# A decoder layer on one core: the last batch's projection, norms, gate and experts tile by tile, in a part of their own behind the slots

## The chip, the core and the metric

The kernel runs on one core of a Trainium2 chip. The core has five engines that run their own instruction streams and meet only through semaphores: PE (TensorE, matrix multiplies into the eight banks of PSUM), DVE (VectorE), ACT (ScalarE), POOL (GpSimd) and SP (SyncE, which here only issues DMAs). The metric is the device time of one execution in microseconds; lower is better.

## The reference

The layer computes, on `x` and `ctx` of 8 batches x 512 tokens x 512 features, a two-part self attention, a cross attention over `ctx`, and a gated pair of experts, each followed by a residual sum and a norm:

```
x = layernorm(x + self_attention(x))
x = layernorm(x + cross_attention(ctx, ctx, x))       # ... @ Wo.T + bo at its end
x = layernorm(x + ffn(x))

def ffn(x):
    weights = softmax(x @ gate_w)                      # 8 experts
    fw, fidx = top_k(weights, 2)
    e0, e1 = silu(x @ w0.T + b0), silu(x @ w1.T + b1)
    return e0 * fw[:, 0:1] * (fidx[:, 0:1] == 0) + e1 * fw[:, 1:2] * (fidx[:, 1:2] == 1)
```

For the change only the last lines of the second step and the third step matter: the output projection of cross attention, the second norm ("ln2"), the gate (8 logits a token, a softmax, and whether expert 0 came first and expert 1 second), the two experts, the third norm ("ln3") and the store.

## The kernel before, in words

The kernel has three phases: self attention, a memory phase, and the cross phase. A batch is four tiles of 128 tokens; attention goes through 32 groups (8 batches x 4 groups of 4 heads), each 16 **slots** long. A slot is one 128x512 block of scores: PE makes it (L1350), ACT takes its exponential (L1569), POOL adds four of them up (L1792), PE weighs the values (L1382); 22 slots ahead PE makes the scores again for the row maxima (L1322), which DVE takes (L1332). All engines' code is written slot by slot by a loop over `CROSS_SLOTS`, and the order on each engine is that of the slots: there is no scheduler.

Everything behind attention is put into the slots of the following batch. `behind(n)` says for slot n which batch has which of its own later steps there: projection from slot 12 of its 64, ln2 applied at 31, transposes at 35, gate at 39, logits at 44, experts from 48 (8 **units**, one for each tile and expert, 3 slots each), ln3's statistics from 62, its factors at 81, applied at 83, stored at 87. These steps share banks 6 and 7; the attention steps use the other six.

The last batch (batch 7) has no attention after it to lie beside. Its steps come in `CROSS_SLOTS` past the 512th slot, where only they and the last steps of batch 6 are left, still in the same slot order and still in banks 6 and 7:

- projection, one tile after another, on PE: a bias matmul (L1429), then four chunks of `cy` by `wo` (L1449, fp32, two instructions a chunk). The last chunk's `cy` is the output of the last group's division on DVE (L1640, L1647). PE waits for it before the first tile
- DVE adds each tile to `cx` (L1667) and takes its statistics (L138, L140). ln2's factors are made by POOL once for all four tiles (L146 to L152), behind the fourth tile's statistics; then ACT applies them to the four tiles (L157)
- transposes on PE (L1461) by feature chunk, each of which needs all four tiles; ACT rounds each to its high part (L1584), DVE takes the low part (L1674)
- gate: the 8 gate columns are the stationary operand, the transposed tokens move (`triple`, L163 to L165, 12 matmuls of 8x512); ACT copies the logits (L1589), PE turns them (L1474), DVE makes masks and weights in 15 small instructions for all four tiles (L1699 to L1735), with an exponential on ACT between them (L1592)
- experts: a unit is a bias matmul and 12 matmuls of 128x512 (L1500). ACT takes tanh (L1598), DVE makes the silu product and with it frees the bank (L1684), ACT weighs it by the gate (L1603), POOL adds it to the tokens (L1772)
- ln3: statistics by tile on DVE, factors for all four tiles on POOL, four applies on ACT (L157), one store of the whole batch, 1024 KB (L1845), and SP's wait for it (L1892).

## Time and profile before

| | us |
|---|---|
| median of three runs | 1899.1 |
| lowest and highest of them | 1894.32, 1899.45 |
| profiled execution, its own time | 1899.85 |
| its span, first to last instruction | 1898.0 |
| PE busy in the span | 1752.7 (92%) |
| DVE, ACT, POOL busy | 1268.1, 973.5, 1084.8 |
| granted clock of PE, mean | 0.966 |

The profile is of one execution. A busy share is an average over the whole span; the digits of the page's 40 slices (47 us each) say that PE is at 9 tenths and more nearly throughout and falls to 6 in the last slice, and the chain that ended last goes through PE for 72% of the span. A row of the timeline gives a start, a duration, the engine, the line and, in brackets, how long the engine stood idle before it and what ended that. The duration of a row with a count is from the first start to the last end. A matmul's duration holds the time that it takes to run through the array, so two that start 0.23 us apart have rows of 0.4 us: the pace is read from starts.

### The profile page before, as it was taken

To read this page: it belongs to the slowest core of one execution; us is meant where nothing else is said; L and a number is where in the kernel's file an instruction comes from. 1 tells how busy PE (TensorE), PEld (TensorE's weight loads), DVE (VectorE), ACT (ScalarE), POOL (GpSimd) and SP (SyncE) were. 2 spreads that over 40 slices of the span, in tenths; PEclk is the share of its full clock that TensorE was granted. 3 is DMA by queue.
4 is the path that set the end of the run, shared out by engine and by line. 5 is a ranking of instruction groups with operands and counts; after the bars stand their busy time and mean duration, and the time that the engine had idled before them with its cause. 6 is when DMAs were issued, how large, how long until landed. Compare 5 with 4: busy or idle time off the path is not lost.

```text
span 1898.0 us, 29834 instructions
## 1 busy us (share of the span) xinstructions
PE 1752.7 (92%) x10442; PEld 1092.6 (58%) x10442; DVE 1268.1 (67%) x2747; ACT 973.5 (51%) x1893; POOL 1084.8 (57%) x741
## 2 busy tenths in 40 slices
PE   5999999999999889999988899999999999999986
PEld 4666666666666467777743355464554546455444
DVE  4677676766767567666867666766677676676632
ACT  3555555555555433333355365655556565555543
POOL 2556455565554645554567567666756756766552
PEclk9999999999999879999989899999999999999998
DMA  6455554554645444566436333444344244343100
GB/s 190 134 156 151 140 157 134 155 153 131 165 124 142 143 159 159 185 191 196 133 119 157 94 95 90 112 117 110 92 117 101 79 117 117 89 102 99 48 23 22
DMA packets 166496, 237.21 MB, mean 125 GB/s; under 512 B 21318, under 2 KB 72518, under 8 KB 166348
## 3 DMA queue, kind: packets, MB, share of 16 engines
q1 hardware_dynamic: 166348, 235.31, 44.7%
q8 instruction: 84, 1.38, 0.3%
q14 instruction: 64, 0.52, 0.1%
HBM read 91.57 MB, written 41.94 MB: 70 GB/s over the span
## 4 chain that ended last, share of the span: by engine, by line
PE 72%; DVE 9%; ACT 5%; DMA 5%; POOL 4%; issue 3%; SPq 2%; POOLq 0%; ACTq 0%; DVEq 0%
PE bank L1500 9%; PE bank L163 7%; PE bank L164 6%; PE bank L165 6%; PE bank L1449 5%; PE bank L1382 5%; PE bank L258 5%; PE bank L1350 5%; PE bank L1322 4%; PE bank L313 4%; PE bank L300 4%; POOL cross_added L1792 3%; DVE bank L1640 2%; PE bank L278 2%; DVE bank L497 2%
## 5 line engine op out<-in xcount | busy, mean ns | idle before, releaser
L1332 DVE TENSOR_REDUCE cross_negmax<-bank 128x1 f32<-128x512 f32 x512 | 342.4, 679 | 213.1 <-PE bank L1322 209.1
L1569 ACT ACTIVATE cpt<-bank 128x512 f32<-128x512 f32 x512 | 299.9, 595 | 214.7 <-PE bank L1350 211.5
L484 DVE CUSTOM_DVE_ANT_0 bank<-bank,future 128x128 f32<-128x128 f32 (+3 forms) x512 | 247.0, 489 | 190.5 <-PE bank L300 189.7
L372 ACT ACTIVATE pt<-bank 128x256 f32<-128x256 f32 (+3 forms) x512 | 219.7, 438 | 269.9 <-PE bank L258 264.7
L1792 POOL TENSOR_TENSOR cross_added<-cross_added,cpt 128x2048 f32<-128x2048 f32 x64 | 292.1, 4565 | 56.4 <-ACT cpt L1569 56.2
L1322 PE MATMUL bank<-cqk 96*128 96x512 f32 x512 | 262.6, 517 | 24.2 <-DMA cqk<-cstage 12.1
L1792 POOL TENSOR_TENSOR cross_added<-cpt,cpt 128x2048 f32<-128x2048 f32 x32 | 146.5, 4578 | 185.9 <-ACT cpt L1569 185.9
L1350 PE MATMUL bank<-cqk 98*128 98x512 f32 x512 | 229.1, 448 | 25.5 <-ACT cpt L1569 18.1
L548 POOL TENSOR_SCALAR_AFFINE_SELECT pt<-pt 128x512 f32<-128x512 f32 x128 | 81.4, 636 | 272.8 <-ACT pt L372 272.7
L258 PE MATMUL bank<-qk 98*128 98x256 f32 (+2 forms) x512 | 182.8, 360 | 20.3 <-ACT pt L372 18.4
L163 PE MATMUL bank<-xt_hi,w_hi 128*128 128x512 f32 x384 | 169.4, 441 | 18.4 <-DVE w_lo L442 15.6
L1350 PEld LDWEIGHTS bank<-cqk 98*128 98x128 f32 x512 | 98.6, 193 | 147.1 <-ACT cpt L1569 68.4
L300 PE MATMUL bank<-qk 96*128 96x256 f32 (+2 forms) x512 | 165.4, 327 | 5.0 <-DMA qk<-stage 4.9
L258 PEld LDWEIGHTS bank<-qk 98*128 98x128 f32 x512 | 97.8, 193 | 99.8 <-ACT pt L372 74.0
L164 PE MATMUL bank<-xt_hi,w_lo 128*128 128x512 f32 x384 | 153.6, 400 | 0.0
L165 PE MATMUL bank<-xt_lo,w_hi 128*128 128x512 f32 x384 | 152.6, 397 | 0.0
L1640 DVE RECIPROCAL bank<-bank 128x128 f32<-128x128 f32 x128 | 121.9, 955 | 41.9 <-PE bank L1415 41.9
L1322 PEld LDWEIGHTS bank<-cqk 96*128 96x128 f32 x512 | 99.3, 196 | 80.6 <-DVE cross_negmax L1332 33.9
L1382 PE MATMUL bank<-cpt,cv 128*32 128x512 f32 x1024 | 140.7, 623 | 0.0
L1449 PE MATMUL bank<-wo,cy 128*128 128x512 f32 x256 | 134.7, 616 | 0.0
L1772 POOL TENSOR_TENSOR x<-x,tanh 128x512 f32<-128x512 f32 x64 | 82.4, 1287 | 85.4 <-ACT tanh L1603 84.3
L497 DVE RECIPROCAL bank<-bank 128x128 f32<-128x128 f32 x128 | 122.1, 958 | 8.8 <-PE bank L278 8.8
(172 smaller groups left out, 3463.8 us busy)
## 6 DMA issues: line engine op xcount, KB each, us to landing
qk<-stage SPq DMA_DIRECT2D x384, 128.0 KB, 2.3
cqk<-cstage SPq DMA_DIRECT2D x384, 128.0 KB, 2.3
scratch_memory<-memory SPq DMA_DIRECT2D x32, 512.0 KB, 3.8
ma<-scratch_memory SPq DMA_DIRECT2D x32, 512.0 KB, 3.9
raw<-in_x_t SPq DMA_DIRECT2D x32, 256.0 KB, 2.7
v<-in_x SPq DMA_DIRECT2D x32, 256.0 KB, 3.3
scratch_y_ar<-y_ar SPq DMA_DIRECT2D x32, 256.0 KB, 2.2
my_ar<-scratch_y_ar SPq DMA_DIRECT2D x32, 256.0 KB, 4.6
```

The costliest lines, as they stand in the source:

```text
L163: pe.matmul(out, a[0], b[0], start=first, stop=False)
L164: pe.matmul(out, a[1], b[0], start=False, stop=False)
L165: return pe.matmul(out, a[0], b[1], start=False, stop=last)
L258: pe.matmul(bank[:, 0:SEQ - q0], kq[0:98, 1, j, first:first + P], kq[0:98, 0, j, q0:SEQ], start=True, stop=True).then_inc(s.pe_st, 1)
L300: pe.matmul(bank[:, 0:max(keys, 256)], kq[0:96, 0, j, tile_of(qt)], kq[0:96, 1, j, 0:max(keys, 256)], start=True, stop=True).then_inc(s.pe ...
L484: dve.tensor_tensor_reduce(out=scores, in0=scores, in1=sh.future[:, SEQ - P * (qt + 1):SEQ], scale=-1.0, scalar=-NEG, op0=ALU.add, op1=ALU ...
L1322: pe.matmul(max_bank(sh, m)[:, :], kq[0:96, 0, jm, tile_of(qt)], kq[0:96, 1, jm, :], start=True, stop=True).then_inc(s.pe_mx, 1)
L1332: dve.reduce_max(s.negmax[gm % 2][:, col:col + 1], max_bank(sh, m)[:, :], AX, negate=True).then_inc(s.dve_max, 1)
L1350: pe.matmul(sh.bank[2 + n % 2][:, :], kq[0:98, 1, j, tile_of(kt)], kq[0:98, 0, j, :], start=True, stop=True).then_inc(s.pe_st, 1)
L1382: done = pe.matmul(sh.bank[4][rows_of(j), :], s.v[g % 2][:, kt, rows_of(j)], s.pt[step % 3][:, j, :], start=(kt == 0), stop=(kt == TILES - ...
L1569: act.activation(s.pt[step % 3][:, j, :], sh.bank[2 + n % 2][:, :], ACT.Exp, scale=SCALE_CROSS).then_inc(s.act_exp, 1)
L1792: pool.tensor_tensor(s.added[:, :, :], old[:, :, :], s.pt[step % 3][:, :, :], ALU.add).then_inc(s.pool_add, 1)
```

## The change

Batch 7 no longer has steps in the slots: `behind` leaves it out, and `CROSS_SLOTS` ends where batch 6 is through (its store). Behind the loop each engine gets a piece of its own for batch 7 (`tail_tensor`, `tail_scalar`, `tail_vector`, `tail_gpsimd`, and the stores in `cross_sync`):

- the projection's four tiles go to banks 0 to 3, and the first two do their first three chunks before their fourth
- adding, statistics, factors (`factors_of_tile`), apply and transposes are per tile; the normed tiles go to a buffer of their own, `x3`, in the place of a key and query stack that is free by then; the transposes use banks 4 and 5, the units banks 6 and 7
- the gate has its operands turned round: the transposed tokens are the stationary operand and the 8 gate columns move, so the logits come out with tokens on partitions, in the bank of that tile's projection. The copy of the logits and their transposes go. There are 12 such matmuls a tile, 48 in all
- the 15 gate instructions on DVE and the exponential on ACT are done for each tile, on a quarter of the columns
- ln3 is per tile, and each tile is stored by itself (256 KB, four stores).

The gate's helpers take a bank, a first tile and a number of tiles now; for the other batches they do what they did. The load of `cx` stands in the same slot as before.

```diff
+    def factors_of_tile(self, pool, b, k):
+        n, ks = 4 * (b + k) + 1, slice(k, k + 1)
+        pool.wait_ge(self.vec, 8 * b + 2 * k + 2)
+        if k == 0:
+            pool.wait_ge(self.applied, TILES * b)
+        pool.tensor_scalar(self.rstd[:, ks], self.mv[:, ks, 1], EPS, None, ALU.add).then_inc(self.root, 1)
+        pool.wait_ge(self.root, n + 1)
+        pool.tensor_tensor(self.rstd[:, ks], self.rstd[:, ks], self.power[:, ks], ALU.pow).then_inc(self.root, 1)
+        pool.wait_ge(self.root, n + 2)
+        pool.tensor_tensor(self.shift[:, ks], self.mv[:, ks, 0], self.rstd[:, ks], ALU.mult).then_inc(self.root, 1)
+        pool.wait_ge(self.root, n + 3)
+        pool.tensor_scalar(self.shift[:, ks], self.shift[:, ks], -1.0, None, ALU.mult).then_inc(self.root, 1)
+    def apply_tile(self, act, b, k, out, r):
+        act.wait_ge(self.root, 4 * (b + k) + 5)
+        act.activation(out, r, ACT.Identity, bias=self.shift[:, k:k + 1],
+                       scale=self.rstd[:, k:k + 1]).then_inc(self.applied, 1)
...
-CROSS_SLOTS = range(SLOTS_BEHIND[LAST + 7][1], NS + 2 * BATCH_SLOTS)
+CROSS_SLOTS = range(SLOTS_BEHIND[LAST + 7][1], NS + 25)
...
+LAST_FREE = (NG - 3) % 3
+        self.x3 = Place(nc, ATTENTION + LAST_FREE * STACK_BYTES, TOP)("x3", [P, TILES, DIM])
...
+LAST_BATCH = BATCH - 1
-    return [(bb, r + more) for bb, more in ((b - 1, 0), (b - 2, BATCH_SLOTS)) if 0 <= bb < BATCH]
+    return [(bb, r + more) for bb, more in ((b - 1, 0), (b - 2, BATCH_SLOTS)) if 0 <= bb < LAST_BATCH]
...
-def cross_gate_first(dve, s, sh, b):
+def cross_gate_first(dve, s, bank, at, k0=0, tiles=TILES):
+    n, ks = GATE_OPS * at, slice(k0, k0 + tiles)
+    logits, beats = gate_scratch(bank, 0, tiles), gate_column(bank, 0, tiles)
...
-    sp.wait_ge(s.out_stored, 16 * BATCH)
+    for k in range(TILES):
+        sp.wait_ge(s.ln3.applied, TILES * LAST_BATCH + k + 1)
+        sp.dma_start(s.t["out"][LAST_BATCH, tile_of(k), :], s.x3[:, k, :]).then_inc(s.out_stored, 16)
+    sp.wait_ge(s.out_stored, 16 * (LAST_BATCH + TILES))
...
+    b = n // BATCH_SLOTS - 1
+    if n % BATCH_SLOTS == 1 and b >= 0:
+        if b >= 1:
+            sp.wait_ge(s.ln2.applied, TILES * b)
+        else:
+            sp.wait_ge(sh.memory_done, 4)
+        sp.wait_ge(second.x1_stored[b % 3], 16 * (b // 3 + 1))
+        sp.dma_start(s.x1[:, :, :], t["x1"][b].rearrange("(k p) d -> p k d", p=P)).then_inc(s.x1_landed, 16)
     for b, slot in behind(n):
-        if slot == 1:
-            if b >= 1:
-                sp.wait_ge(s.ln2.applied, TILES * b)
-            else:
-                sp.wait_ge(sh.memory_done, 4)
-            sp.wait_ge(second.x1_stored[b % 3], 16 * (b // 3 + 1))
-            sp.dma_start(s.x1[:, :, :], t["x1"][b].rearrange("(k p) d -> p k d", p=P)).then_inc(s.x1_landed, 16)
...
+def tail_tensor(pe, s, cw, sh):
+    pe.wait_ge(s.act_exp, NS)
+    pe.wait_ge(s.dve_max, NS)
+    for k in (0, 1):
+        tail_project(pe, s, cw, sh, k, range(GROUPS - 1))
+    for k in (0, 1):
+        tail_project(pe, s, cw, sh, k, (GROUPS - 1,))
+    tail_project(pe, s, cw, sh, 2, range(GROUPS))
+    tail_transposed(pe, s, sh, 0)
+    tail_project(pe, s, cw, sh, 3, range(GROUPS))
+    tail_transposed(pe, s, sh, 1)
+    for k in range(TILES):
+        tail_gate(pe, s, cw, sh, k)
+        for i in range(2):
+            tail_expert(pe, s, cw, sh, 2 * k + i)
+        if k + 2 < TILES:
+            tail_transposed(pe, s, sh, k + 2)
+def tail_project(pe, s, cw, sh, k, chunks):
+    b = LAST_BATCH
+    for c in chunks:
+        if c == 0:
+            cross_bias(pe, cw, sh.bank[k], 0)
+        pe.wait_ge(s.dve_norm, (TILES + 1) * (GROUPS * b + c + 1))
+        done = pe.matmul(sh.bank[k][:, :], s.y[:, (GROUPS * b + c) % (GROUPS + 1), tile_of(k)], cw.wo[:, c, :],
+                         start=False, stop=(c == GROUPS - 1))
+        if c == GROUPS - 1:
+            done.then_inc(s.pe_po, 1)
+def tail_transposed(pe, s, sh, k):
+    pe.wait_ge(s.ln2.applied, TILES * LAST_BATCH + k + 1)
+    if k == 0:
+        pe.wait_ge(s.act_raw, NG)
+    elif k == 1:
+        pe.wait_ge(s.dve_norm, (TILES + 1) * NG)
+    else:
+        pe.wait_ge(s.dve_x2t, GROUPS * LAST_BATCH + k - 1)
+    for c in range(GROUPS):
+        done = pe.transpose(sh.bank[4 + k % 2][:, tile_of(c)], s.x3[:, k, tile_of(c)], sh.ident[:, :])
+    done.then_inc(s.pe_x2t, 1)
+def tail_gate(pe, s, cw, sh, k):
+    pe.wait_ge(s.dve_x2t, GROUPS * LAST_BATCH + k + 1)
+    pe.wait_ge(s.dve_po, TILES * LAST_BATCH + k + 1)
+    for c in range(GROUPS):
+        done = triple(pe, sh.bank[k][:, 0:EXPERTS], (s.x2t_hi[:, c, tile_of(k)], s.x2t_lo[:, c, tile_of(k)]),
+                      (cw.gate_hi[:, c, :], cw.gate_lo[:, c, :]), c == 0, c == GROUPS - 1)
+    done.then_inc(s.pe_gate, 1)
+def tail_expert(pe, s, cw, sh, u):
+    k, i = divmod(u, 2)
+    bank = sh.bank[6 + u % 2]
+    pe.wait_ge(s.dve_u, UNITS * LAST_BATCH + u - 1)
+    cross_bias(pe, cw, bank, 1 + i)
+    for c in range(GROUPS):
+        done = None
+        for x, w in ((s.x2t_hi, s.e_hi), (s.x2t_lo, s.e_hi), (s.x2t_hi, s.e_lo)):
+            done = pe.matmul(bank[:, :], x[:, c, tile_of(k)], w[:, i, c, :], start=False,
+                             stop=(c == GROUPS - 1 and w is s.e_lo))
+    done.then_inc(s.pe_ex, 1)
+def tail_scalar(act, s, sh):
+    b = LAST_BATCH
+    act.wait_ge(s.pe_st, NS)
+    act.wait_ge(s.pe_mx, NS)
+    for k in range(TILES):
+        s.ln2.apply_tile(act, b, k, s.x3[:, k, :], s.x1[:, k, :])
+        if k in (1, 2):
+            tail_high(act, s, sh, k - 1)
+    for k in range(TILES):
+        act.wait_ge(s.dve_gate, GATE_OPS * (b + k) + GATE_FIRST)
+        act.activation(gate_scratch(sh.bank[k], 1, 1), s.ge[:, k:k + 1, :], ACT.Exp).then_inc(s.act_gate, 1)
+        tail_tanh(act, s, sh, 2 * k)
+        tail_weigh(act, s, 2 * k)
+        tail_tanh(act, s, sh, 2 * k + 1)
+        if k + 2 < TILES:
+            tail_high(act, s, sh, k + 2)
+        if k >= 1:
+            s.ln3.apply_tile(act, b, k - 1, s.x3[:, k - 1, :], s.x3[:, k - 1, :])
+        tail_weigh(act, s, 2 * k + 1)
+    s.ln3.apply_tile(act, b, TILES - 1, s.x3[:, TILES - 1, :], s.x3[:, TILES - 1, :])
+def tail_high(act, s, sh, k):
+    act.wait_ge(s.pe_x2t, GROUPS * LAST_BATCH + k + 1)
+    if k == 0:
+        act.wait_ge(s.pe_ex, UNITS * LAST_BATCH)
+    act.activation(s.x2t_hi[:, :, tile_of(k)], sh.bank[4 + k % 2][:, :].rearrange("p (c q) -> p c q", q=P),
+                   ACT.Copy).then_inc(s.act_x2t, 1)
+def tail_tanh(act, s, sh, u):
+    n = UNITS * LAST_BATCH + u
+    act.wait_ge(s.pe_ex, n + 1)
+    act.wait_ge(s.pool_x2, n - 1)
+    act.activation(s.tanh[u % 2][:, :], sh.bank[6 + u % 2][:, :], ACT.Tanh, scale=0.5).then_inc(s.act_tanh, 1)
+def tail_weigh(act, s, u):
+    k, i = divmod(u, 2)
+    act.wait_ge(s.dve_u, UNITS * LAST_BATCH + u + 1)
+    act.wait_ge(s.dve_gate, GATE_OPS * (LAST_BATCH + k + 1))
+    act.activation(s.tanh[i][:, :], s.tanh[i][:, :], ACT.Copy, scale=s.w[i][:, k:k + 1]).then_inc(s.act_w, 1)
+def tail_vector(dve, s, sh):
+    b = LAST_BATCH
+    dve.wait_ge(s.x1_landed, 16 * (b + 1))
+    for k in range(TILES):
+        dve.wait_ge(s.pe_po, TILES * b + k + 1)
+        dve.tensor_tensor(s.x1[:, k, :], sh.bank[k][:, :], s.x1[:, k, :], ALU.add).then_inc(s.dve_po, 1)
+        dve.wait_ge(s.dve_po, TILES * b + k + 1)
+        s.ln2.statistics(dve, b, k, s.x1[:, k, :])
+        if k >= 2:
+            tail_low(dve, s, sh, k - 2)
+    for k in range(TILES):
+        dve.wait_ge(s.pe_gate, b + k + 1)
+        cross_gate_first(dve, s, sh.bank[k], b + k, k, 1)
+        cross_gate_weights(dve, s, sh.bank[k], b + k, UNITS * b, k, 1)
+        tail_silu(dve, s, sh, 2 * k)
+        if k >= 1:
+            tail_statistics(dve, s, k - 1)
+        tail_silu(dve, s, sh, 2 * k + 1)
+        if k + 2 < TILES:
+            tail_low(dve, s, sh, k + 2)
+    tail_statistics(dve, s, TILES - 1)
+def tail_low(dve, s, sh, k):
+    dve.wait_ge(s.act_x2t, GROUPS * LAST_BATCH + k + 1)
+    dve.tensor_tensor(s.x2t_lo[:, :, tile_of(k)], sh.bank[4 + k % 2][:, :].rearrange("p (c q) -> p c q", q=P),
+                      s.x2t_hi[:, :, tile_of(k)].bitcast(F32), ALU.subtract).then_inc(s.dve_x2t, 1)
+def tail_silu(dve, s, sh, u):
+    tanh = s.tanh[u % 2]
+    dve.wait_ge(s.act_tanh, UNITS * LAST_BATCH + u + 1)
+    dve.scalar_tensor_tensor(out=tanh[:, :], in0=tanh[:, :], scalar=1.0, in1=sh.bank[6 + u % 2][:, :],
+                             op0=ALU.add, op1=ALU.mult).then_inc(s.dve_u, 1)
+def tail_statistics(dve, s, k):
+    dve.wait_ge(s.pool_x2, UNITS * LAST_BATCH + 2 * k + 2)
+    s.ln3.statistics(dve, LAST_BATCH, k, s.x3[:, k, :])
+def tail_gpsimd(pool, s):
+    b = LAST_BATCH
+    for k in range(TILES):
+        s.ln2.factors_of_tile(pool, b, k)
+    for u in range(UNITS):
+        x = s.x3[:, u // 2, :]
+        pool.wait_ge(s.act_w, UNITS * b + u + 1)
+        pool.wait_ge(s.pe_x2t, GROUPS * b + u // 2 + 1)
+        if u % 2 == 1:
+            pool.wait_ge(s.pool_x2, UNITS * b + u)
+        pool.tensor_tensor(x, x, s.tanh[u % 2][:, :], ALU.add).then_inc(s.pool_x2, 1)
+        if u >= 2 and u % 2 == 0:
+            s.ln3.factors_of_tile(pool, b, u // 2 - 1)
+    s.ln3.factors_of_tile(pool, b, TILES - 1)
```

PE, from the projection of batch 7 to its first expert. Before (`cy` attention output by chunk, `x_176` the normed tokens, `exp_hi` and `x2t_hi` weights and transposed tokens):

```order
L1429 MATMUL bank<-bias_rows,bias_ones 128x512 [waits dve_cross_norm,dve_u]
L1449 MATMUL bank<-wo,cy 128x512 x4
...
L1429 MATMUL bank<-bias_rows,bias_ones 128x512 [waits dve_cross_norm,dve_po]
L1449 MATMUL bank<-wo,cy 128x512 x4
L1461 MATMUL bank<-ident,x_176 128x128 [waits dve_po,ln2_applied]
L1461 MATMUL bank<-ident,x_176 128x128 x3
...
L163 MATMUL bank<-x2t_hi,gate_hi 8x512 [waits dve_x2t]
...
L1474 MATMUL bank<-ident,logits_t 128x8 [waits dve_x2t,act_lt]
L1474 MATMUL bank<-ident,logits_t 128x8 x3
L1429 MATMUL bank<-bias_rows,bias_ones 128x512 [waits act_lt]
```

The same place in the changed kernel (`x_177` is `x3`):

```order
L1459 MATMUL bank<-bias_rows,bias_ones 128x512 [waits dve_cross_max,act_cross_exp]
L1951 MATMUL bank<-wo,cy 128x512 [waits dve_cross_norm] x3
L1459 MATMUL bank<-bias_rows,bias_ones 128x512
L1951 MATMUL bank<-wo,cy 128x512 [waits dve_cross_norm] x5
L1459 MATMUL bank<-bias_rows,bias_ones 128x512
L1951 MATMUL bank<-wo,cy 128x512 [waits dve_cross_norm] x4
L1966 MATMUL bank<-ident,x_177 128x128 [waits act_cross_raw,ln2_applied]
L1966 MATMUL bank<-ident,x_177 128x128 x3
...
L1966 MATMUL bank<-ident,x_177 128x128 [waits dve_cross_norm,ln2_applied]
...
L182 MATMUL bank<-gate_hi,x2t_hi 128x8 [waits dve_po,dve_x2t]
```

The first tile's transposes stand between the third and the fourth tile's projection, and the gate and two units of a tile follow before the next-but-one tile is transposed.

ACT, from the last tile's exponential on. Before:

```order
L1598 ACTIVATE tanh_161<-bank 128x512 [waits pool_x2,pe_ex]
L1603 ACTIVATE tanh_161<-tanh_161,gate_w_172 128x512 [waits dve_gate,dve_u]
L1598 ACTIVATE tanh_162<-bank 128x512 [waits pool_x2,pe_ex]
L1603 ACTIVATE tanh_162<-tanh_162,gate_w_173 128x512 [waits dve_gate,dve_u]
L157 ACTIVATE x_176<-x_176,ln_shift,ln_rstd 128x512 [waits ln3_root]
L157 ACTIVATE x_176<-x_176,ln_shift,ln_rstd 128x512 x3
```

The changed kernel:

```order
L2004 ACTIVATE bank<-gate_exp 128x8 [waits dve_gate]
L2028 ACTIVATE tanh_161<-bank 128x512 [waits pool_x2,pe_ex]
L2035 ACTIVATE tanh_161<-tanh_161,gate_w_172 128x512 [waits dve_gate,dve_u]
L2028 ACTIVATE tanh_162<-bank 128x512 [waits pool_x2,pe_ex]
L170 ACTIVATE x_177<-x_177,ln_shift,ln_rstd 128x512 [waits ln3_root]
L2035 ACTIVATE tanh_162<-tanh_162,gate_w_173 128x512 [waits dve_gate,dve_u]
L170 ACTIVATE x_177<-x_177,ln_shift,ln_rstd 128x512 [waits ln3_root]
```

The apply of the tile before, with its wait for POOL's factors, now stands between the last unit's tanh and its weighing.

## Rows read from the trace of the kernel before

**Rows 1.** Stages of the end: length, busy us (instructions) by engine, clock, DMA share

```profile
1828.00:1843.00 15.00, 14.89 (x36) 6.75 (x36) 6.71 (x14) 3.65 (x5) 2.96 (x5) 1.00 0.18 70
1843.00:1849.70 6.70, 0.00 (x0) 0.00 (x0) 1.57 (x3) 2.92 (x4) 1.70 (x4) 0.74 0.00 0
1849.70:1852.00 2.30, 1.97 (x8) 1.57 (x8) 0.40 (x1) 0.84 (x3) 0.00 (x0) 0.50 0.00 0
...
1884.00:1898.00 14.00, 0.00 (x0) 0.00 (x0) 2.35 (x5) 4.24 (x6) 3.38 (x6) 0.61 0.19 75
```

**Rows 2.** Timeline of PE, from the last unit of batch 6 to the last matmul

```profile
1826.40 0.40 PE L1500 MATMUL bank<-exp_lo,x2t_hi 128*128 128x512 f32 x1
1828.09 0.47 PE L1429 MATMUL bank<-bias_rows,bias_ones 128*128 128x512 f32 x1 [1.30 <-DVE cy L1647]
1831.43 0.79 PE L1429 MATMUL bank<-bias_rows,bias_ones 128*128 128x512 f32 x1
...
1835.09 0.79 PE L1429 MATMUL bank<-bias_rows,bias_ones 128*128 128x512 f32 x1
...
1862.67 0.39 PE L1429 MATMUL bank<-bias_rows,bias_ones 128*128 128x512 f32 x1
...
1883.58 0.40 PE L1500 MATMUL bank<-exp_lo,x2t_hi 128*128 128x512 f32 x1
```

**Rows 3.** Timeline of PE, short matmuls at full clock, in earlier stages

```profile
703.80 0.60 PE L869 MATMUL bank<-ident,my_ar 128*128 128x128 f32 x4
...
707.70 0.83 PE L836 MATMUL bank<-e,ka_t 128*128 128x128 f32 x6
...
1111.10 0.41 PE L1474 MATMUL bank<-ident,logits_t 8*128 8x8 f32 x4
```

**Rows 4.** Timeline of DVE: fourth add, first and last gate instruction, last statistics

```profile
1843.02 0.69 DVE L1667 TENSOR_TENSOR cx<-bank,cx 128x512 f32<-128x512 f32 x1 [2.02 <-PE bank L1449]
...
1859.65 0.19 DVE L1699 TENSOR_REDUCE gate_max<-bank 128x4 f32<-128x32 f32 x1 [3.98 <-PE bank L1474]
...
1861.83 0.23 DVE L1735 TENSOR_TENSOR gate_w<-bank,gate_keep 128x4 f32<-128x4 f32 x2
...
1887.46 0.69 DVE L138 BATCH_NORM_STATS2 ln_stats<-x 128x6 f32<-128x512 f32 x1 [1.31 <-POOL x L1772]
```

**Rows 5.** Timeline of ACT: ln2, gate, last unit, ln3

```profile
1846.78 2.93 ACT L157 ACTIVATE x<-cx,ln_shift,ln_rstd 128x512 f32<-128x512 f32 x4 [8.17 <-POOL ln_shift L152]
...
1860.89 0.20 ACT L1592 ACTIVATE bank<-gate_exp 128x32 f32<-128x32 f32 x1 [1.74 <-DVE gate_keep L1716]
...
1884.01 0.60 ACT L1598 ACTIVATE tanh<-bank 128x512 f32<-128x512 f32 x1 [0.94 <-PE bank L1500]
1885.36 0.72 ACT L1603 ACTIVATE tanh<-tanh,gate_w 128x512 f32<-128x512 f32 x1 [0.76 <-DVE tanh L1684]
1890.44 2.92 ACT L157 ACTIVATE x<-x,ln_shift,ln_rstd 128x512 f32<-128x512 f32 x4 [4.36 <-POOL ln_shift L152]
```

**Rows 6.** Timeline of POOL: last adds of batch 6 and 7, ln3's factors

```profile
1829.38 1.26 POOL L1772 TENSOR_TENSOR x<-x,tanh 128x512 f32<-128x512 f32 x1 [1.73 <-ACT tanh L1603]
...
1883.14 1.28 POOL L1772 TENSOR_TENSOR x<-x,tanh 128x512 f32<-128x512 f32 x1 [1.73 <-ACT tanh L1603]
1886.16 1.26 POOL L1772 TENSOR_TENSOR x<-x,tanh 128x512 f32<-128x512 f32 x1 [1.74 <-ACT tanh L1603]
1888.46 0.23 POOL L146 TENSOR_SCALAR ln_rstd<-ln_mv 128x4 f32<-128x4 f32 x1 [1.03 <-DVE ln_mv L140]
1888.77 1.04 POOL L148 TENSOR_TENSOR ln_rstd<-ln_rstd,ln_power 128x4 f32<-128x4 f32 x1
```

**Rows 7.** SP's last wait (line, releaser: total, times, longest us)

```profile
SPq L1892 <- DMA out<-x: 3.8, 1, 3.8
```

**Rows 8.** DMA issues: KB each, median us from issue to landing

```profile
scratch_y_ar<-y_ar SPq DMA_DIRECT2D x32, 256.0 KB, 2.2
...
out<-x SPq DMA_DIRECT2D x8, 1024.0 KB, 5.1
```

68 lines of the change are left out of this document (35 added, 33 removed).

## The prediction

> **What bounds the kernel now.** The page of the profile comes first: PE is busy throughout and falls off only in the last of its 40 slices, so the change works in the one stretch where PE is not the whole answer. I then cut that stretch into stages by the windows view [rows 1] and followed each engine's timeline through them [rows 2, 4 to 6]. The reader should see a row of stages in single file. PE projects four tiles back to back. Then it does nothing for 6.70 us, while DVE, POOL and ACT make ln2 for all four tiles one after another, and its clock falls: 0.74 of full in that stage, 0.50 in the next, which is the lower of its two levels, 1.2 GHz [rows 1]. Transposes, gate and logits follow, each waiting for a copy by another engine, the first part of them at that level. Only from the first unit (its second bias matmul is at 1862.67) does PE run without a gap again, to the last matmul at 1883.58 [rows 2]. Behind that come 14 us in which PE does nothing: the last unit's tanh, silu, weighing, add and statistics, ln3 for four tiles, one store.
>
> **Paces.** A matmul's row holds about 0.17 us that the next one need not wait for: the last one is 0.40 long, while 7 units of 13 matmuls take 1883.58 + 0.23 - 1862.67 = 21.14 us, so 3.02 a unit and 0.23 a matmul [rows 2]. A projected tile takes 1835.09 - 1831.43 = 3.66 us: a bias matmul of 0.23 and four chunks of 0.86. Without the 0.17, six matmuls of 128x128 in 0.83 us and four transposes in 0.60 us come to 0.11 us each, and four 8x8 ones to 0.06 [rows 3].
>
> **PE's part of the change.** In the changed kernel PE goes from the last matmul of batch 6 (1826.40 + 0.23 = 1826.63) straight to the bias and the first three chunks of tiles 0 and 1. These need only `cy` chunks that are done, and so cover the 1.30 us that PE waits for DVE's last division now [rows 2].
> - Projection: 4 x 3.66 = 14.64 us, the same work. The fourth chunk of tile 0 is through at 1826.63 + 2 x (0.23 + 3 x 0.86) + 0.86 = 1833.1.
> - ln2 of tile 0: now the fourth add starts 0.29 us after PE's last chunk (1828.09 + 14.64 = 1842.73 against 1843.02), and the first apply 3.76 us after the add's start (1846.78) [rows 2, 4, 5]. So the add of tile 0 is at 1833.4, its apply at 1837.15 and done by 1837.95 (2.93 us for four, 0.73 each, and a little for a lone one [rows 5]). ACT must be through with ln3 of batch 6 by then: its last add ends at 1829.38 + 1.26 = 1830.64; from the end of such an add to the applies it is 3.02 us (1887.42 to 1890.44), and the applies take 2.92, so 1836.6 [rows 5, 6]. That holds by half a microsecond. PE reaches tile 0's transposes at 1837.6 and waits 0.35 us. For tiles 1 to 3 the same chain runs beside PE's work.
> - Transposes: 16, at 0.11 us: 1.76.
> - Gate, the one item that grows. Twelve matmuls of 8x512 for the batch become 48 that load 128 columns of weights to move 8. The trace has none such with these weights. From below, the 8x8 matmuls bound it: 48 x 0.06 = 2.9 us. From above, a matmul that moves 512 columns: 48 x 0.23 = 11.0 us. I take 0.11, the pace of matmuls that load as wide a weight and move 128 columns, since the load is what is left when hardly anything moves: 5.28 us.
> - Units: 8 x 3.02 = 24.16 us.
> - The logits' copy and turn, and the waits between transposes and gate: gone.
>
> Sum: 14.64 + 0.35 + 1.76 + 5.28 + 24.16 = 46.19 us, so PE is through at 1872.82, its last result at 1872.99 instead of 1883.98 (1883.58 + 0.40). **11.0 us earlier.**
>
> **Does anything else hold PE up?** A unit needs its bank back: tanh and silu of the unit two before, some 1.4 us after its end, while the bank is wanted 3.02 us after it. For each tile PE takes 0.44 + 1.32 + 6.04 = 7.8 us. DVE has the gate (1859.65 to 1862.06 for 15 instructions, 2.4 us; they are small, so I give a quarter of the columns the same time), two silus, a statistic and a low part: about 5.4 us [rows 4]. ACT has about 4.2 us, and a wait. POOL has two adds (1.3 each) and factors of 1.98 us (1888.46 to 1890.44) [rows 5, 6]. All are below 7.8, so the four-fold gate costs DVE 7 us more and PE nothing: it lies beside units.
>
> **The end behind the last matmul.** Let E be its end. Now: tanh at E + 0.03, weighing at E + 1.38, add at E + 2.18, statistics at E + 3.48, ln3's four applies from E + 6.46 to E + 9.38 [rows 4 to 6]. One apply instead of four saves 2.92 - 0.75 = 2.17 us. But the change writes a wait into ACT's order: tanh of the last unit, then the apply of tile 2, then the weighing of the last unit. The apply needs factors that POOL makes behind the add of unit 6. That add ends at E + 0.44 (1883.14 + 1.28); factors take 1.98, so the apply runs from E + 2.42 to E + 3.17, and what queues behind it is the weighing, and behind that POOL's add and everything that ends the kernel. The gate of tile 3 makes unit 6 later still: ACT's exponential stands behind the same kind of wait for the tile before, so the gate's weights are there about 0.15 us after the silu could start. The weighing comes at about E + 3.35, 1.97 us late. The last apply ends at E + 9.38 + 1.97 - 2.17 = E + 9.18: **0.2 us** of the 2.17 are left.
>
> POOL's power is 1.04 us for four columns [rows 6]. For one column it lies between 0.23 (its neighbour's time) and 1.04; twice on this path, it could give up to 1.6 us. I take 1.04, the same operation's own row.
>
> **The last store.** From the last apply's end (1893.36) to the span's end it is 4.64 us, 3.8 of them SP's wait for 1024 KB [rows 5, 7]. A 256 KB store of the same form takes 2.2 us to land in mid-kernel, where 1024 KB take 5.1 [rows 8]. At the quiet end it may be 2.2 x 3.8 / 5.1 = 1.6, and 3.8 if size did nothing. With 2.2: **1.6 us** saved. The three earlier stores lie beside the units.
>
> **Total**: 11.0 + 0.2 + 1.6 = 12.8 us. The profiled execution took 1899.85 us, which gives 1887.05 (a span of 1885.2). It is 0.75 us above the median of three, 1899.1, so the forecast for the median is 1886.3 us.
>
> **The rivals.**
> - *The gate runs at the pace of wide matmuls* (a narrow one of this type may have a floor that no row shows). 5.7 us more: 1892.0. Against it, 128x128 and 8x8 ones run at 0.11 and 0.06 [rows 3].
> - *DVE and ACT become the bound in the tile loop.* ACT's 4.2 us and its wait of about 1.9 leave 1.7 us of PE's 7.8. If small instructions and the round trip DVE, ACT, DVE cost more than in the batch, banks come free late. One microsecond a tile: 4 us, 1890.3.
> - *The clock falls, on the other side of zero.* PE's clock was at the lower level after a wait of 6.7 us and not after one of 1.30, since the stage that follows has 1.00 [rows 1, 2]. The changed tail has no long wait, but between the tiles' units it has 16 short matmuls in a row, 1.8 us of work that keeps the array little busy. If the clock falls there and a unit of each tile runs at half pace, that is 4 x 3.02 = 12.1 us: 1898.4, no change. If it falls at the first gate and stays, the units take 24.2 us more: 1910.5. It decides the sign once more than 12.8 us of full-pace work runs at half.
>
> On this the Trainium skill speaks against the change: "TensorE: Matmul & The Clock Gate", section "Part 4: PE-mode transpose", says that transposes do not count as busy for the clock in the same way, and its section "Why this matters for your kernels" warns of thin matmuls. By that rule the last rival is what happens, 1898.4 or more instead of 1886.3. The trace bears it out in part: the transposes of [rows 1] ran at 0.50, but behind a long wait.
>
> **How the numbers follow.** The forecast has 0.70. The gate at wide pace 0.11, DVE and ACT as the bound 0.09, the clock for a unit a tile 0.05, the clock for good 0.03, other causes 0.02, half each of no change and slower. The low end takes the bounds below (gate 2.4, power 1.6, store 0.6: 1881.7), the high end the first rival and the store that saves nothing (1892.0 + 1.6 = 1893.6), so 1881.5 to 1893.5. A measurement of this kernel can tell about 0.3%, 5.7 us, from no change. Faster by more: 0.70 + 0.11 + 0.09 = 0.90. Within it 0.06, slower 0.04.
>
> **What would show it.** PE's timeline: no gap of 1.30 before the projection, about 0.35 before the first transposes, 12 gate matmuls in some 1.3 us, units at 3.02, clock 1.00 from 1828 to the last matmul near 1873. ACT's: the apply of tile 2 about 2.4 us behind the last unit's end, waiting for POOL, with the last weighing behind it. SP's last wait near 2.2 us. It is wrong if units are longer than 3.02, if PE waits for DVE between units, or if the slots before 1826 changed.

## The result and the profile after

| | kernel before | changed kernel |
|---|---|---|
| median of six runs | 1899.74 us (1894.32 to 1903.37) | 1881.92 us (1876.57 to 1889.08) |
| ratio, 95% interval | 1 | 0.9902 (0.9883 to 0.9921) |
| profiled execution | 1899.85 us | 1885.54 us |
| its span | 1898.0 us | 1883.4 us |

The changed kernel is faster by 1.0%. On the 1899.1 us from which the forecast was made, the ratio gives 1880.5 us (1876.9 to 1884.1): 5.8 under the forecast of 1886.3, and 1.0 below the low end of its range. The direction was right, the gain was larger than forecast, and the range was too narrow on that side. The medians alone give a little less, 1881.92 / 1899.74 = 0.9906. (Three executions of the later comparisons took 4336, 5584 and 7675 us; they are in no ratio and no median of this text.)

The stages of the changed end, in the windows view of the changed kernel: stretch, its length, busy us (instructions) of PE, PE's weight loads, DVE, ACT and POOL, granted clock, DMA share, GB/s.

```profile
1826.80:1837.80 11.00, 11.00 (x28) 4.95 (x28) 6.60 (x13) 5.06 (x7) 6.06 (x12) 1.00 0.00 1
1837.80:1843.60 5.80, 5.80 (x30) 3.79 (x29) 3.65 (x6) 2.71 (x4) 1.62 (x6) 1.00 0.46 178
1843.60:1857.90 14.30, 14.30 (x73) 11.89 (x73) 7.55 (x38) 5.62 (x11) 4.74 (x7) 1.00 0.00 1
1857.90:1873.00 15.10, 14.98 (x79) 12.38 (x77) 8.27 (x39) 7.28 (x14) 7.47 (x13) 1.00 0.09 35
1873.00:1883.40 10.40, 0.00 (x0) 0.00 (x0) 1.56 (x3) 2.75 (x4) 4.02 (x10) 0.68 0.13 50
```

Against [rows 1]: in the first four stretches PE's busy time is the whole length (in the fourth the last 0.12 us lies behind its last matmul), and the clock is 1.00 up to there. The 6.70 us without a matmul and the stages at 0.74 and 0.50 are gone.

PE's timeline of the changed kernel (start, length, engine, line, operation, out<-in, tile, count), against [rows 2]:

```profile
1826.61 0.40 PE L1530 MATMUL bank<-exp_lo,x2t_hi 128*128 128x512 f32 x1
1826.85 0.40 PE L1459 MATMUL bank<-bias_rows,bias_ones 128*128 128x512 f32 x1
...
1837.84 0.60 PE L1966 MATMUL bank<-ident,x 128*128 128x128 f32 x4
...
1842.30 0.25 PE L182 MATMUL bank<-gate_hi,x2t_hi 128*128 128x8 f32 x1
...
1843.64 0.48 PE L1459 MATMUL bank<-bias_rows,bias_ones 128*128 128x512 f32 x1
...
1846.76 0.39 PE L1459 MATMUL bank<-bias_rows,bias_ones 128*128 128x512 f32 x1
...
1872.48 0.40 PE L1988 MATMUL bank<-exp_lo,x2t_hi 128*128 128x512 f32 x1
```

No row between the first and the last has an idle time in brackets. Twelve gate matmuls take 1843.64 - 1842.30 = 1.34 us, so 0.11 each; the first unit of tile 0 takes 3.12 us, where 3.02 was the mean of a unit before.

What follows PE's last matmul, in the changed kernel's timelines of ACT, of POOL, and SP's last wait (total, times, longest us), against [rows 5 to 7]:

```profile
1872.92 0.60 ACT L2028 ACTIVATE tanh<-bank 128x512 f32<-128x512 f32 x1 [0.90 <-PE bank L1988]
1874.93 0.81 ACT L170 ACTIVATE x<-x,ln_shift,ln_rstd 128x512 f32<-128x512 f32 x1 [1.42 <-POOL ln_shift L166]
1875.65 0.70 ACT L2035 ACTIVATE tanh<-tanh,gate_w 128x512 f32<-128x512 f32 x1
1880.21 0.81 ACT L170 ACTIVATE x<-x,ln_shift,ln_rstd 128x512 f32<-128x512 f32 x1 [3.85 <-POOL ln_shift L166]
```

```profile
1873.74 0.57 POOL L162 TENSOR_TENSOR ln_rstd<-ln_rstd,ln_power 128x1 f32<-128x1 f32 x1
```

```profile
SPq L2104 <- DMA out<-x: 1.6, 1, 1.6
```

The wait that the prediction named is there: ACT's second row is the apply of tile 2, waiting for POOL, and the weighing of the last unit comes behind it. POOL's power takes 0.57 us for one column, and SP's wait for the last store 1.6 us.

I call the stretch from the end of batch 6's last unit to the end of the span the **tail**. Up to it, the order of the instructions is the same in both kernels, on every engine, and the two traces hold the same instructions up to there. Before, it runs from 1826.63 to 1898.0, 71.4 us; now from 1826.85 to 1883.4, 56.55 us. So the change shortened it by 14.8 us, where 12.8 were forecast. The medians are 17.8 us apart (1899.74 - 1881.92). Two questions were left: where the 2 us come from, and where the other 3.

### The profile page after: what moved, and what is told of

The parts are those of the page before. It is cut to its first block, busy times and chain, and to the rows that moved or that the text cites. A ratio compares the mean times of both kernels' runs of the same rounds, so it can differ in the third digit from the quotient of the medians.

```text
span 1883.4 us, 29983 instructions
## 1 busy us (share of the span) xinstructions
PE 1753.0 (93%) x10474; PEld 1096.4 (58%) x10474; DVE 1274.1 (68%) x2792; ACT 972.2 (52%) x1895; POOL 1087.9 (58%) x765
## 4 chain that ended last, share of the span: by engine, by line
PE 73%; DVE 8%; ACT 5%; DMA 4%; POOL 4%; issue 3%; SPq 2%; POOLq 0%; ACTq 0%; DVEq 0%
PE bank L1530 8%; PE bank L182 7%; PE bank L183 6%; PE bank L184 6%; PE bank L277 5%; PE bank L1412 5%; PE bank L1380 5%; PE bank L332 4%; PE bank L1351 4%; PE bank L1479 4%; PE bank L319 4%; POOL cross_added L1826 3%; PE bank L297 2%; DVE bank L516 2%; DVE bank L1672 2%
## 5 line engine op out<-in xcount | busy, mean ns | idle before, releaser
L1826 POOL TENSOR_TENSOR cross_added<-cross_added,cpt 128x2048 f32<-128x2048 f32 x64 | 292.2, 4566 | 55.1 <-ACT cpt L1600 54.7
L182 PEld LDWEIGHTS bank<-xt_hi,w_hi 128*128 128x128 f32 x384 | 73.8, 192 | 89.8 <-issue 73.7
L581 POOL TENSOR_TENSOR self_added<-self_added,pt 128x1024 f32<-128x1024 f32 x64 | 117.4, 1835 | 5.3
```

Of the source, the lines that this page charges most:

```text
L182: pe.matmul(out, a[0], b[0], start=first, stop=False)
L1826: pool.tensor_tensor(s.added[:, :, :], old[:, :, :], s.pt[step % 3][:, :, :], ALU.add).then_inc(s.pool_add, 1)
```

## The experiments

The theories. For the terms of the tail: each part of the change gives what the rows priced (the narrow power, the small store, no wait on PE), and a part that is taken back returns just that. For the 3 us outside the tail, **S** says that they are scatter, and **U** that the changed kernel also runs something faster ahead of it. For the rival that decided the sign, the clock, one theory says that only a wait of PE brings it down, and another that short matmuls in a row do so without one.

one_store, whole_tiles, gate_twice and gate_spread have a single execution each, the profiled one (1887.23, 1884.79, 1904.92 and 1890.57 us); they are read by their tails alone. In the table, the start of PE's last matmul, the end of the last apply and the end of the span (the tail) are counted from the tail's start, in us.

| kernel | tail starts | last matmul | last apply's end | tail |
|---|---|---|---|---|
| before | 1826.63 | 56.95 | 66.7 | 71.4 |
| before_again | 1826.37 | 56.8 | 66.6 | 71.1 |
| changed | 1826.85 | 45.6 | 54.2 | 56.55 |
| after_again | 1822.17 | 45.55 | 54.1 | 56.5 |
| after_third | 1828.17 | 45.6 | 54.2 | 56.6 |
| apply_behind | 1821.29 | 45.5 | 52.7 | 55.1 |
| norm_together | 1828.93 | 55.6 | 64.2 | 66.6 |
| norm_filled | 1823.96 | 54.9 | 63.4 | 65.8 |
| one_store | 1826.42 | 45.5 | 54.1 | 58.7 |
| whole_tiles | 1824.66 | 47.1 | 55.6 | 58.0 |
| gate_twice | 1834.56 | 57.2 | 65.8 | 68.1 |
| gate_spread | 1825.04 | 51.1 | 60.9 | 63.4 |
| last_on_dve | 1820.52 | 45.6 | 51.5 | 53.9 |
| last_on_dve_b | 1830.82 | 45.6 | 51.5 | 53.9 |

### Both kernels again: is the rest scatter?

No edit: the kernel before against itself, and the changed kernel twice more.

> The kernel before once more, as a control. Two theories on why the medians moved by 17.8 us where the two profiles differ by 14.5 (span 1898.0 to 1883.4). Theory S (scatter): all engines have the same instructions in the same order up to the tail, so what exceeds the tail's 14.5 us is scatter of runs in the part ahead of the tail, in the waits and the granted clock of the memory phase (660 to 1000 us). Then this kernel against itself gives a ratio within 0.2% of 1, with single runs several us apart, and the start of batch 7's projection (1828.09 in the first profile) moves by as much as the span does. Theory U (upstream): the changed kernel is faster ahead of the tail too, by some 3 us, by where its code or a buffer lies. Then the projection starts at 1828 in every profile of this kernel and earlier, near 1823, in those of the changed one.

> The changed kernel once more. Theory S: the ratio is 0.990 to 0.993 (14.5 us is 0.9924), the tail from the first projection (1826.85 in its first profile) to the end of the span is 56.5 us again within 0.3, whatever the span is, and the start of the tail moves with the clock of the memory phase. Theory U: ratio 0.990 or less and a tail that starts near 1823.

> The changed kernel a third time, for its ratio beside last_on_dve on one chip. Theory S (the gain is the tail's 14.8 us, the rest scatter ahead of it): ratio 0.992, tail 56.5 us. Theory U (3 us more ahead of the tail): 0.990.

The kernel before against itself: 1.0001 (0.9985 to 1.0016). The changed kernel: 0.9913 (0.9893 to 0.9933) and 0.9919 (0.9902 to 0.9936). Its tail is 56.5 and 56.6 us, within 0.1 of the first trace, and the kernel before has 71.1 in its second. So the 14.8 us repeat, and the first ratio was the largest gain of three. Their mean is 0.9911, 16.9 us; the tail alone gives 1 - 14.8 / 1899 = 0.9922.

The scatter lies ahead of the tail. In 12 traces of kernels whose order up to there is the same, the tail starts between 1820.5 and 1834.6, at 1826.1 in the mean; in the two traces of before at 1826.63 and 1826.37. Most of it arises between 580 and 1080 us, in and around the memory phase: counted along PE's matmuls, all 14 traces are within 2.2 us of each other at the 3000th (577 to 579 us), within 12.8 at the 7000th (1068 to 1081 us), and within 14.0 just ahead of the tail. The latest of them, gate_twice, has a granted clock of 0.94 from 400 to 800 us and 0.93 from 800 to 1000, the earliest, last_on_dve, 0.96 and 0.95. In the changed kernel's six runs the shorter times have the higher mean clock (1876.57 and 1877.94 us have 0.973, 1889.08 has 0.966), but that does not hold run by run: in after_third 1883.05 us has 0.975 and 1881.92 has 0.971. So the clock goes with the scatter; that it is its whole cause isn't shown. Over the eight comparisons of several runs each (the changed kernel's three, and those of apply_behind, norm_together, norm_filled and last_on_dve below), the ratio is 0.0006 lower in the mean than the shortened tail would give, 1.2 us. U's 3 us are not there, and in the traces the tail does not start earlier in the changed kernel; whether a systematic 1 us is, these runs can't tell.

### ACT's order: the apply behind the weighing

```
         if k + 2 < TILES:
             tail_high(act, s, sh, k + 2)
+        tail_weigh(act, s, 2 * k + 1)
         if k >= 1:
             s.ln3.apply_tile(act, b, k - 1, s.x3[:, k - 1, :], s.x3[:, k - 1, :])
-        tail_weigh(act, s, 2 * k + 1)
```

> The changed kernel with ln3's apply of the tile before put behind the second unit's weighing on ACT instead of ahead of it. Theory W (the written wait): the last weighing waits for POOL's factors of tile 2, from 1.38 to 2.76 us behind the last matmul's end, and everything behind it is late by that. Then the last weighing comes at E + 1.4, the last apply ends at E + 6.8 instead of E + 8.13 (E the last matmul's end), and the kernel is 1.3 us faster than the changed one, ratio to the kernel before about 0.001 lower. Rival: POOL is the limit, its factors of tile 2 and the last add share the engine, and the last add starts no earlier than E + 2.5: gain 0.3 us or none.

ACT's timeline of apply_behind, with PE's last result at 1866.83 + 0.40 = 1867.23:

```profile
1868.62 0.72 ACT L2035 ACTIVATE tanh<-tanh,gate_w 128x512 f32<-128x512 f32 x1 [0.75 <-DVE tanh L2070]
1869.30 0.81 ACT L170 ACTIVATE x<-x,ln_shift,ln_rstd 128x512 f32<-128x512 f32 x1
1873.20 0.81 ACT L170 ACTIVATE x<-x,ln_shift,ln_rstd 128x512 f32<-128x512 f32 x1 [3.09 <-POOL ln_shift L166]
```

The weighing comes at E + 1.39 instead of E + 2.77, and the last apply ends at E + 6.78 instead of E + 8.14: 1.36 us, and the tail is 1.4 us shorter. The new wait in ACT's order was real and had its price, though less than the 1.97 us forecast, since the factors of one column are quicker. The ratio, 0.9922 (0.9898 to 0.9946), can't show 1.4 us.

### One store of the batch

```
-    for k in range(TILES):
-        sp.wait_ge(s.ln3.applied, TILES * LAST_BATCH + k + 1)
-        sp.dma_start(s.t["out"][LAST_BATCH, tile_of(k), :], s.x3[:, k, :]).then_inc(s.out_stored, 16)
-    sp.wait_ge(s.out_stored, 16 * (LAST_BATCH + TILES))
+    sp.wait_ge(s.ln3.applied, TILES * BATCH)
+    sp.dma_start(s.t["out"][LAST_BATCH].rearrange("(k p) d -> p k d", p=P), s.x3[:, :, :]).then_inc(s.out_stored, 16)
+    sp.wait_ge(s.out_stored, 16 * BATCH)
```

> The changed kernel with one store of 1024 KB for batch 7 instead of four of 256 KB. It tells what the store by tile is worth. The prediction said 1.6 us, from 2.2 us against 3.8; the trace of the changed kernel shows a last wait of 1.6 us. Size theory: the last wait is 3.8 us again, and the tail is 58.7 us instead of 56.5. Rival: the shorter last wait comes from the quiet end and not from the size; then the last wait stays at 1.6 to 2 and the tail under 57.

SP's last wait in one_store:

```profile
SPq L2103 <- DMA out<-x: 3.8, 1, 3.8
```

It is 3.8 us again, as in [rows 7], and the tail 2.2 us longer (58.7 against 56.5; 58.7 was expected), with the last apply's end where it was. The term of the store is its size: 2.2 us, where 1.6 were forecast.

### Tiles 0 and 1 projected whole

```
+    pe.wait_ge(s.dve_norm, (TILES + 1) * NG)
     for k in (0, 1):
-        tail_project(pe, s, cw, sh, k, range(GROUPS - 1))
-    for k in (0, 1):
-        tail_project(pe, s, cw, sh, k, (GROUPS - 1,))
+        tail_project(pe, s, cw, sh, k, range(GROUPS))
```

> The changed kernel with the first two tiles projected whole, one after the other, behind the last group's division, as the kernel before did. It tells what the three chunks ahead are worth. Cover theory: PE waits 1.2 to 1.3 us for cy (it waited 1.30 in the kernel before), so the tail, counted from the end of batch 6's last unit, is 57.5 us instead of 56.5: 1.3 for the wait, less 0.3, since tile 0's fourth chunk comes 1.7 us earlier against 1.3 later and its norm lies fully beside PE. Rival: the wait is moved to the first transposes anyway and it costs nothing.

PE's timeline of whole_tiles:

```profile
1824.43 0.40 PE L1530 MATMUL bank<-exp_lo,x2t_hi 128*128 128x512 f32 x1
1826.12 0.47 PE L1459 MATMUL bank<-bias_rows,bias_ones 128*128 128x512 f32 x1 [1.30 <-DVE cy L1679]
```

The wait of [rows 2] is back to the hundredth, the tail is 1.5 us longer (58.0, where 57.5 were expected), and the clock stays at 1.00. By its starts PE loses 1826.12 - 1824.66 = 1.46 us here, and that is the whole of it: nothing later makes up for it, and nothing is lost behind it.

### ln2 for four tiles together, with and without a filled wait

norm_together projects all four tiles, then makes ln2's factors for them at once:

```
     tail_project(pe, s, cw, sh, 2, range(GROUPS))
+    tail_project(pe, s, cw, sh, 3, range(GROUPS))
     tail_transposed(pe, s, sh, 0)
-    tail_project(pe, s, cw, sh, 3, range(GROUPS))
     tail_transposed(pe, s, sh, 1)
...
-        s.ln2.apply_tile(act, b, k, s.x3[:, k, :], s.x1[:, k, :])
+        s.ln2.apply(act, b, k, s.x3[:, k, :], s.x1[:, k, :])
...
-    for k in range(TILES):
-        s.ln2.factors_of_tile(pool, b, k)
+    s.ln2.factors(pool, b)
```

> The changed kernel with ln2's factors of batch 7 made once for all four tiles, so that all four projections come first and every transpose waits for the fourth tile's statistics. It tells what of the 11 us on PE is the wait and its clock. Theory K (wait and clock): PE stops at about 1841.3 (first projection at 1826.85 and four tiles of 3.66), the first apply starts 4.05 us later and ends at 1846.2, so a wait of 4.8 us where 0.1 was; the tail grows by 4.8 and, if the clock falls to the lower level in it as it did before, by up to 3 us more. So 4.8 to 8 us slower than the changed kernel, ratio to the kernel before 0.993 to 0.996. Rival: the tile-wise norm matters little because POOL, ACT and DVE are in the way later, and it costs under 2 us.

norm_filled is the same, and has PE work in its wait, on a bank that nobody uses (20 matmuls of 128x512, about the time of the wait):

```
+    pe.wait_ge(s.dve_u, UNITS * LAST_BATCH)
+    for _ in range(20):
+        pe.matmul(sh.bank[7][:, :], cw.row_ones[:, :], cw.rows[:, 0, :], start=True, stop=True)
     tail_transposed(pe, s, sh, 0)
```

> norm_together (one set of ln2 factors for four tiles) with 20 matmuls of 128x512 into an idle bank in PE's wait, 4.66 us of work that nothing uses. It tells the wait from the clock. norm_together's tail, from the first projection to the end of the span, took 66.6 us in its trace, the changed kernel's 56.5. Theory K (two parts): 4.7 us of these 10.0 are the wait itself and 5.3 the lower clock behind it, through the transposes, the first gate and most of two units. Then the filled wait keeps the clock at 1.00 and the tail is 61.3 us, a saving of 5 us by work that does nothing. Rival: the clock falls all the same, or what is slow behind the wait is slow for another reason (banks, the order of transposes and low parts), and the tail stays at 66.

The windows of norm_together behind the projection, and PE's rows in them:

```profile
1848.00:1854.00 6.00, 5.01 (x21) 4.61 (x22) 1.66 (x6) 3.57 (x6) 0.00 (x0) 0.51 0.00 0
1854.00:1860.00 6.00, 6.00 (x19) 4.64 (x19) 1.81 (x14) 0.78 (x2) 0.00 (x0) 0.64 0.00 0
```

```profile
1848.43 1.97 PE L1966 MATMUL bank<-ident,x 128*128 128x128 f32 x8 [4.68 <-ACT x L176]
1853.54 0.77 PE L1459 MATMUL bank<-bias_rows,bias_ones 128*128 128x512 f32 x1
1858.83 0.40 PE L1459 MATMUL bank<-bias_rows,bias_ones 128*128 128x512 f32 x1
```

The tail is 10.0 us longer than the changed kernel's, all of it ahead of PE's last matmul; 4.8 to 8 were expected. 4.7 us are the wait. Behind it the lower level costs 2.2 in the first unit (5.29 us instead of 3.12), 1.2 in the gate (2.58 instead of 1.34) and 0.6 in the eight transposes (1.97 against 1.36 at full pace, as norm_filled below shows), 4.0 together; the rest of the other 5.3 is waits among them and the order. The ratio is 0.9978 (0.9962 to 0.9994). So making ln2 tile by tile is what carries most of the gain.

In norm_filled PE's rows and windows are these:

```profile
1838.21 5.10 PE L1937 MATMUL bank<-bias_rows,bias_ones 128*128 128x512 f32 x20
1843.46 1.36 PE L1969 MATMUL bank<-ident,x 128*128 128x128 f32 x8
1845.53 0.27 PE L182 MATMUL bank<-gate_hi,x2t_hi 128*128 128x8 f32 x1 [0.71 <-DVE x2t_lo L2066]
...
1846.56 0.36 PE L182 MATMUL bank<-gate_hi,x2t_hi 128*128 128x8 f32 x1
...
1847.20 0.77 PE L1459 MATMUL bank<-bias_rows,bias_ones 128*128 128x512 f32 x1
...
1852.89 0.62 PE L1459 MATMUL bank<-bias_rows,bias_ones 128*128 128x512 f32 x1
```

```profile
1843.00:1848.00 5.00, 4.10 (x24) 3.21 (x23) 2.00 (x9) 3.59 (x6) 0.00 (x0) 0.85 0.00 0
1848.00:1854.00 6.00, 6.00 (x16) 4.65 (x16) 1.38 (x10) 0.78 (x2) 0.00 (x0) 0.55 0.01 3
```

This expectation failed: 61.3 us of tail were expected with the clock kept up, and it is 65.8, only 0.7 less than without the filling (the ratio is 0.9959, 0.9944 to 0.9975). The filling did keep it up through the wait: the eight transposes ran at full pace (1.36 us against 1.97), and so did nine gate matmuls. Then, with PE at work, the tenth took 0.36 us instead of 0.25, and the first unit took 5.69. What PE had done before that was eight transposes, a wait of 0.71 and nine gate matmuls. So a long wait is not needed, and the lower level behind norm_together's wait can't be put down to the wait alone: that order also sets eight transposes, a short wait and the gate in a row. That made the last rival of the prediction, which the changed kernel had not shown, a question again.

### The gate's matmuls doubled: in a row, and spread

gate_twice issues the gate's sum twice over in tail_gate, so 24 short matmuls a tile; the second sum starts from zero again and takes the place of the first. Ahead of the gates of tiles 0, 1 and 2 stand four transposes (those of the next tile); the gate of tile 3 comes straight behind a unit.

```
-    for c in range(GROUPS):
+    for c in 2 * tuple(range(GROUPS)):
```

> The changed kernel with each tile's 12 gate matmuls done twice over (the second set starts the sum again, so the logits are the same). 48 more matmuls that load 128 columns and move 8. Price theory: 0.11 us each, all on PE's path, so the tail grows by 5.3 us to 61.9. Clock rival: with 28 short matmuls in a row between units the granted clock falls, units take longer than 3.02 us, and the tail grows by more than 8. Cover rival: PE waits for the other engines anyway, and the tail grows by less than 4.

gate_spread issues the same 24, by twos behind each of the 12 wide matmuls of the tile's first unit (the sum is started again here too):

```
         for x, w in ((s.x2t_hi, s.e_hi), (s.x2t_lo, s.e_hi), (s.x2t_hi, s.e_lo)):
             done = pe.matmul(bank[:, :], x[:, c, tile_of(k)], w[:, i, c, :], start=False,
                              stop=(c == GROUPS - 1 and w is s.e_lo))
+            for a, g, first, last in gate[:2]:
+                short = pe.matmul(sh.bank[k][:, 0:EXPERTS], a, g, start=first, stop=last)
...
+            gate = gate[2:]
```

> gate_twice with its 24 gate matmuls of a tile put by twos between the 12 wide matmuls of the tile's first unit, instead of in a row ahead of it. gate_twice's tail took 68.1 us: 5.3 more than the changed kernel for the 48 short matmuls and 6.3 more because the granted clock fell in each tile. Row theory: it falls because 28 short matmuls (4 transposes and 24 of the gate) stand in a row, 3.1 us in which the array does little; spread, the same number leaves it at 1.00 and the tail takes 61.8 us, at most 1.5 more for the gate's results, which come a unit later. Count theory: the number of short matmuls or the gate's part of the time is what counts, the clock falls all the same, and the tail takes 66 or more.

The windows of gate_twice around the first unit of tile 0 and the second, and PE's rows of these two units' starts:

```profile
1845.50:1852.70 7.20, 7.20 (x43) 5.19 (x42) 4.40 (x8) 2.71 (x4) 2.59 (x9) 1.00 0.37 144
1852.70:1857.30 4.60, 4.60 (x15) 3.65 (x15) 1.76 (x15) 0.99 (x2) 0.25 (x2) 0.63 0.00 0
1857.30:1860.40 3.10, 3.10 (x15) 2.43 (x15) 0.69 (x1) 1.33 (x2) 0.69 (x1) 1.00 0.02 5
```

```profile
1852.70 0.48 PE L1459 MATMUL bank<-bias_rows,bias_ones 128*128 128x512 f32 x1
1857.35 0.39 PE L1459 MATMUL bank<-bias_rows,bias_ones 128*128 128x512 f32 x1
```

PE has no wait here, and the clock still falls: 0.63 in the first unit of tile 0, which takes 4.65 us instead of 3.12, and 1.00 again in the second. (0.63 is a mean of both levels; from its sixth matmul to its last, starts are 0.43 us apart instead of 0.23.) It is so for each tile (4.65 or 4.66 us four times), and for tile 3 without a transpose in the row:

```profile
1881.55 0.40 PE L1988 MATMUL bank<-exp_lo,x2t_hi 128*128 128x512 f32 x1
1881.79 0.17 PE L182 MATMUL bank<-gate_hi,x2t_hi 128*128 128x8 f32 x1
...
1884.38 0.67 PE L1459 MATMUL bank<-bias_rows,bias_ones 128*128 128x512 f32 x1
1889.03 0.39 PE L1459 MATMUL bank<-bias_rows,bias_ones 128*128 128x512 f32 x1
```

Between the unit's last matmul at 1881.55 and the next unit's bias matmul at 1884.38 lie the 24 gate matmuls and nothing else, 2.6 us; the unit behind them takes 4.65. The tail is 11.6 us longer: 48 matmuls at 0.11 are 5.3, and the four units' 1.53 each are 6.1. This is the prediction's rival of the clock for a unit a tile, at twice the dose of gate matmuls; it had 3.02 us a unit for it, 12.1 in all, so half as much came.

The windows of gate_spread over the same part, and its first unit of tile 0:

```profile
1845.00:1850.00 5.00, 5.00 (x28) 4.21 (x28) 2.36 (x16) 1.52 (x4) 0.02 (x1) 1.00 0.00 0
1850.00:1860.00 10.00, 10.00 (x62) 8.73 (x60) 4.88 (x21) 3.97 (x8) 3.43 (x3) 1.00 0.01 2
```

```profile
1840.49 0.48 PE L1459 MATMUL bank<-bias_rows,bias_ones 128*128 128x512 f32 x1
1846.18 0.48 PE L1459 MATMUL bank<-bias_rows,bias_ones 128*128 128x512 f32 x1
```

The same 24 short matmuls, and the clock is 1.00 up to PE's last matmul. The unit that holds them takes 5.69 us: 3.12 and 24 at 0.107. PE's last matmul is 5.5 us later than in the changed kernel, which is the doubled gate's own 5.3 and little else. So here it is the row of short matmuls that brings the clock down, not their number in a tile. The spreading isn't free: the gate's weights come a unit later, and the last apply ends at E + 9.4 instead of E + 8.14, which gives the tail of 63.4; 61.8 to 63.3 were expected.

### A version for less time: the last unit weighed and added by DVE

From apply_behind; for the last unit alone, DVE multiplies by the gate's weight and adds in one instruction, in place of ACT's weighing and POOL's add.

```
-    tail_statistics(dve, s, TILES - 1)
+    x = s.x3[:, TILES - 1, :]
...
+    dve.scalar_tensor_tensor(out=x, in0=s.tanh[1][:, :], scalar=s.w[1][:, TILES - 1:TILES], in1=x,
+                             op0=ALU.mult, op1=ALU.add).then_inc(s.dve_last, 1)
+    dve.wait_ge(s.dve_last, 1)
+    s.ln3.statistics(dve, b, TILES - 1, x)
...
-    for u in range(UNITS):
+    for u in range(UNITS - 1):
```

> The changed kernel with the apply behind the weighing, and the last unit's weighing and add made by DVE in one instruction (the product times the gate weight plus the tokens, 0.69 us) instead of ACT's 0.72 and POOL's 1.27 with two hand-overs. Counted from E, the last matmul's end: silu done at E + 1.35, the new instruction to E + 2.05, statistics to E + 3.0, POOL's factors of the last tile (1.3) to E + 4.4, apply to E + 5.25, where the changed kernel has E + 8.13 and apply_behind E + 6.78. Tail 53.6 us instead of 56.5. Rival: the chain behind the last matmul isn't what ends the kernel, an earlier store or an engine in its tail is; then the tail stays above 55.

> last_on_dve a second time, beside the changed kernel. Its tail was 53.9 us against 56.5. Ratio to the kernel before 0.0014 below that of the changed kernel, 0.990 to 0.991 under theory S, tail 53.9 us. Rival: its first ratio, 0.9906, was luck of the runs ahead of the tail, and it is no faster than the changed kernel.

DVE's timeline of last_on_dve, with PE's last result at 1866.56: silu, the new instruction, and the statistics behind it.

```profile
1867.22 0.69 DVE L2079 SCALAR_TENSOR_TENSOR tanh<-tanh,bank 128x512 f32<-128x512 f32 x1 [1.47 <-ACT tanh L2030]
1867.94 0.75 DVE L2064 SCALAR_TENSOR_TENSOR x<-tanh,gate_w,x 128x512 f32<-128x512 f32 x1
1868.73 0.69 DVE L138 BATCH_NORM_STATS2 ln_stats<-x 128x6 f32<-128x512 f32 x1
```

One instruction of 0.75 us stands for a weighing of 0.72, an add of 1.26 and two hand-overs. The last apply ends at E + 5.45, and the tail is 53.9 us in both traces (53.6 were expected), 2.7 shorter than the changed kernel's: 1.4 of that is ACT's order, as in apply_behind, and 1.2 the new instruction. The ratios to the kernel before are 0.9906 (0.9881 to 0.9932) and 0.9897 (0.9877 to 0.9918), with medians of 1881.66 and 1881.47 us, where the changed kernel had 1881.92, 1883.10 and 1883.57. It beats the kernel before; that it beats the changed one is shown by the traces of the tail and not by the times, which can't tell 2.7 us.

## Why the prediction was wrong where it was

The direction and the mechanism were right: PE's stages in single file became PE without a wait, and the written wait of ACT stood where it was said. What failed are three terms. POOL's power was taken at 1.04 us for one column and took 0.57. The last store was taken at 2.2 us and took 1.6. And the range gave nothing for the scatter of the runs, which was put at nothing without a reason. The first two make 2.0 us of the miss of 5.8; the other 3.8 are not in the tail.

- **PE, 11.0 us forecast, 11.3 measured** in the tail's own time: 46.03 us from its start to the last result against 57.35. The 0.35 us of wait ahead of the first transposes did not come, as the apply of tile 0 started 0.46 us sooner than worked out (1836.91 against 1837.15 + 0.22): that is POOL's power for one column again, 0.58 us there. By PE's starts, projection took 14.75 us (14.64 forecast), the transposes 1.40 (1.76), the gate 5.27 (5.28) and the units 24.44 (24.16). The gate, the one term between bounds of 2.9 and 11.0, was well taken at 0.11 us a matmul. A unit behind short matmuls takes 3.1 us and not the mean of 3.02; the first unit before took 1862.67 - 1859.54 = 3.13, a row that the prediction left out of its mean.
- **The end behind the last matmul, 0.2 forecast, 1.2 measured**: the last apply ends at E + 8.14, where E + 9.18 was forecast and E + 9.38 stood before. This term was mis-sized by the value taken for POOL's power, 1.04 us for one column, where the row shows 0.57. Factors of a tile stand twice on this path, 1.48 us each instead of 1.98 (1873.45 to 1874.93, 1878.73 to 1880.21), which is the whole miss of 1.0 us; the first puts tile 2's apply at E + 2.05 and not at E + 2.42, and the weighing at E + 2.77 and not at E + 3.35.
- **The store, 1.6 forecast, 2.3 measured**: 2.38 us from the last apply's end to the span's end instead of 4.64, SP's wait 1.6 instead of 2.2. The scaled estimate of the prediction (2.2 x 3.8 / 5.1 = 1.6) was the right one, and the value from mid-kernel was taken.
- **Sum**: 11.3 + 1.2 + 2.3 = 14.8 us.
- **The range.** Its low end took the bounds of three terms, 1881.7 less a little, and gave nothing for the medians themselves. The tail as it came gives 1899.1 - 14.8 = 1884.3, inside the range. The ratio that was measured lies 3.8 us below that, and the first ratio was the furthest of three: 0.9902, where 0.9913 and 0.9919 would have been 1882.6 and 1883.7 us, inside the range. In the first two traces the tail starts at 1826.63 and 1826.85, so nothing ahead of it was faster; how the other runs of that comparison got their 3.8 us has no trace, and scatter is the reading that the repeats leave. One kernel's ratio moved by 0.0017 here, 3.2 us, and its medians from 1881.92 to 1883.57. The prediction had a 5.7 us limit for its chances and left it out of the range.
- **Rivals.** The gate at wide pace: no. DVE and ACT as the bound: no; PE has no wait from 1826.85 to its last matmul, though the gate of one tile takes DVE 2.9 us (1844.28 to 1847.15 with a wait for ACT) and not 2.4. The clock: not here, at 4 transposes and 12 gate matmuls in a row (12 alone ahead of the last tile's units), where the windows show 1.00; in all eight traces of that order PE's last matmul comes 45.5 or 45.6 us into the tail (47.1 in whole_tiles, with its own 1.5). But the chance of 0.08 was given on weak ground. With 12 more in the row it came in each tile and took 6.1 us, beside the 5.3 that these matmuls cost themselves, from a gain of 14.8. "TensorE: Matmul & The Clock Gate" of the Trainium skill, section "Part 4: PE-mode transpose", says of transposes that they do not count as busy in the same way. No run here tells how they count. What the runs show is that they are not needed: for tile 3 of gate_twice 24 matmuls that are no transposes were followed by the lower level, and the transposes of the changed kernel were not.

## What to carry to other kernels

When the end of a kernel is stages of a whole batch in single file, cut them by tile: most of the gain was the norm between projection and experts, whose wait cost 4.7 us by itself; 4.0 more were lost at the lower clock behind it, and filling the wait did not bring that back. Short matmuls made by such a cut belong between wide ones if there are many in a row; and an instruction that waits for a side chain does not go ahead of the one that the end hangs on. Price each operation at its new width, and give a range the scatter of the medians beside the bounds of the terms.

## What the runs showed of the hardware

- The clock can fall with PE never idle: in gate_twice 4 transposes and 24 matmuls of 128x8 in a row take 3.0 us (for the last tile the 24 alone, 2.6 us), and the next 4.6 us are at 0.63; in gate_spread the same matmuls by twos between wide ones leave it at 1.00. One trace each, four tiles in each.
- A filled wait is no cure by itself: in norm_filled the clock held through the wait and fell among the short matmuls behind it, at 1846.56, where the filling had ended at 1843.31.
- POOL's power takes 1.04 us for four columns and 0.57 for one; its neighbour (L146, now L160) takes 0.23 us for four and 0.21 for one.
- A matmul of 128-column weights that moves 8 columns starts every 0.11 us, the pace of those in [rows 3] that move 128.
- SP's last wait for a store: 3.8 us for 1024 KB (before and one_store), 1.6 for 256 KB (the changed kernel).
